# Turning weights and the first token pairs in 64-row halves, with another prologue order

## The reference

```python
x + attention(xn, ...) + ffn(xn, ...)
# ffn: one scalar per token and channel m (64 of them), 16 inner units each
s = xn @ Win + bin_                                  # [tokens, 64]
h = relu(s[..., None] * W1 + b1)                     # [tokens, 64, 16]
g = einsum('btmh,mh->btm', h, W2) + b2
ffn = g @ Wout + bout
# attention: q, k, v = projections of a second layer norm of xn (Wq, Wk, Wv),
# 16 heads of 32; its loops slice [:, :, :16], the first 16 tokens of each batch.
# Three rounds of: ql, kl, vl = small 32x32 projections of q, k, v; layer norms of
# ql and kl; softmax(ql kl^T); out = that @ vl; q += out; k, v = kl, vl.
attention = out.transpose(...).reshape(...) @ Wo.T + bo
```

## Time and profile before

| | |
|---|---|
| median of 3 runs (lowest, highest) | 303.13 us (302.8, 304.87) |
| profiled execution: its time, its span | 303.48 us, 301.7 us |
| busy: TensorE, VectorE, ScalarE, POOL | 276.4, 251.3, 219.9, 234.0 us |
| share of the span | 92%, 83%, 73%, 78% |
| DMA | 87.87 MB, mean 291 GB/s |
| mean granted TensorE clock | 0.979 |

### The profile page before, as it was taken

How to read it: one execution, slowest core, us unless ns; L and a number is a source line. 1 busy time by engine, 2 the same in 40 slices (tenths; PEclk the granted TensorE clock), 3 DMA queues, 4 the chain that set the end, 5 groups by cost and what they waited for, 6 DMA issues and landing times.

```text
span 301.7 us, 6220 instructions
## 1 busy us (share of the span) xinstructions
PE 276.4 (92%) x2371; PEld 116.1 (38%) x2371; DVE 251.3 (83%) x392; ACT 219.9 (73%) x260; POOL 234.0 (78%) x209
## 2 busy tenths in 40 slices
PE   4797498989999999899999999999989999999990
PEld 4652265524443432434443434434343333242220
DVE  0878484999997799998599987899999989967682
ACT  1546733873788699797979778898769797976910
POOL 8543109999679797979897897979793989899940
PEclk9999689997999999999999999999999999999998
...
GB/s 239 284 369 393 255 189 333 342 347 285 262 302 250 238 360 290 389 283 386 194 319 296 335 343 294 357 267 406 171 357 302 354 314 333 126 233 37 240 241 336
DMA packets 50573, 87.87 MB, mean 291 GB/s; under 512 B 6360, under 2 KB 35184, under 8 KB 46448
## 3 DMA queue, kind: packets, MB, share of 16 engines
...
...
## 4 chain that ended last, share of the span: by engine, by line
PE 61%; DVE 23%; issue 6%; POOL 3%; DMA 3%; ACT 1%; DVEq 0%; POOLq 0%; ACTq 0%
PE sg L594 14%; PE sg L537 13%; PE op L629 12%; DVE x L1048 6%; DVE stats L1092 5%; PE ra L556 4%; PE ra L629 3%; DMA b2c<-in_L_ffn_b_dram 3%; DVE xqT L1079 2%; PE op L352 2%; PE rb L483 1%; PE op L483 1%; PE ra L483 1%; PE ra L352 1%; PE A L326 1%
## 5 line engine op out<-in xcount | busy, mean ns | idle before, releaser
L1227 POOL TENSOR_TENSOR x<-x,bias_row 128x512 f32<-128x512 f32 x128 | 160.5, 1293 | 0.0
L1092 DVE BATCH_NORM_STATS2 stats<-x 128x6 f32<-128x512 f32 x128 | 80.7, 672 | 9.5 <-DMA x<-in_L_attn_x_dram 9.5
L816 ACT ACTIVATE H<-ra,b1c,w1c 128x1024 f32<-128x1024 f32 x64 | 72.8, 1205 | 9.4 <-PE rb L556 9.3
L816 ACT ACTIVATE H<-rb,b1c,w1c 128x1024 f32<-128x1024 f32 x60 | 68.9, 1220 | 3.0 <-PE sg L594 2.5
L594 PE MATMUL sg<-H,w2s 128*32 128x512 f32 x496 | 64.6, 616 | 3.0 <-ACT H L816 2.9
L1048 DVE TENSOR_TENSOR x<-x,op 128x1024 f32<-128x1024 f32 x46 | 55.7, 1212 | 13.3 <-PE op L629 13.2
L1211 POOL TENSOR_TENSOR rstd<-veps,nhalf 128x8 f32<-128x8 f32 x16 | 26.7, 1671 | 43.0 <-DVE veps L1104 42.9
L537 PE MATMUL sg<-xT,win 128*32 128x512 f32 x256 | 58.0, 595 | 1.3 <-ACT xqT L787 0.9
L629 PE MATMUL op<-wout,G 64*128 64x512 f32 x184 | 51.6, 637 | 2.2 <-DVE x L1048 1.9
L537 PE MATMUL sg<-xqT,winq 128*32 128x512 f32 x224 | 50.8, 595 | 0.0
L1079 DVE STREAM_TRANSPOSE xqT<-xq 128x1024 f32<-128x1024 f32 x28 | 34.6, 1234 | 2.2 <-DMA xq<-in_L_attn_x_dram 2.1
...
## 6 DMA issues: line engine op xcount, KB each, us to landing
out_dram<-x SPq DMA_DIRECT2D x30, 1024.0 KB, 6.8
...
x<-in_L_attn_x_dram SPq DMA_DIRECT2D x12, 1024.0 KB, 11.9
...
x<-in_L_attn_Wq_dram SPq DMA_DIRECT2D x1, 1024.0 KB, 19.0
x<-in_L_attn_Wk_dram SPq DMA_DIRECT2D x1, 1024.0 KB, 21.1
x<-in_L_attn_Wv_dram SPq DMA_DIRECT2D x1, 1024.0 KB, 7.4
```

The source lines that it names most:

```text
L816: act.activation(Hr[half][k % len(Hr[half])][:, :], rep_ps[half][:, :], ACT.Relu, bias=b1c[:, half, k:k + 1], scale=w1c[:, half, k:k + 1]) ...
L1092: dve.bn_stats(stats[:, j, :], x_sb[m][:, j * D:(j + 1) * D]).then_inc(bn_done, 1)
L1227: pool.tensor_tensor(x_sb[m][:, c], x_sb[m][:, c], bias_row[:, :], ALU.add).then_inc(xc_done, 1)
```

## The change

The four weights are loaded into x4 and x5 (Wq, Wk; Wv, Wo). The buffers WvT and WoT take the turned Wq and Wk first, and after `product_qk` the turned Wv and Wo. A unit now is eight tiles in sixteen 64-row halves, written to two banks (o_ps or RA_ps in turn); VectorE copies the first bank, ScalarE the second, for unit 0 VectorE both. There are 8 units instead of 16, and `product_qk` follows the fourth. `turn_first` turns the first two pairs the same way, four units for a pair, and `evacuate_first` copies 1024 columns at once.

The load of pair 3 waits for nothing any more, that of pair 4 for four units, that of pair 5 for eight. SP issues quads(2) and pair 3 right behind Wo. Thirteen small loads (bq, bv; three 32x32 weights, five vectors, three scalars) are issued by POOL: two between inv_std(0) and inv_std(1), eleven between inv_std(1) and inv_std(2). In the last attention round the kT product and its copy are left out, since nothing reads them. The tables of places are new, and VectorE takes the first three statistics of pair 4 one pair earlier, as it does from pair 5 on. The diff, its core:

```diff
-        w_nat = [x_sb[3 + i // 2 * 2][:, (i % 2) * DC * D:(i % 2 + 1) * DC * D].rearrange("p (c i) -> p c i", c=DC) for i in range(4)]
-        w_t = [t.rearrange("p (c o) -> p c o", c=DC) for t in
-               (x_sb[4][:, 0:DC * D], x_sb[4][:, DC * D:2 * DC * D], sb("WvT", [P, DC * D])[:, :], sb("WoT", [P, DC * D])[:, :])]
+        w_nat = [x_sb[4 + i // 2][:, (i % 2) * DC * D:(i % 2 + 1) * DC * D].rearrange("p (c i) -> p c i", c=DC) for i in range(4)]
+        w_t = [t[:, :].rearrange("p (c o) -> p c o", c=DC) for t in (sb("WvT", [P, DC * D]), sb("WoT", [P, DC * D]))]
+        w_t = w_t + w_t
...
+            if n == 4 and h == 0:
+                sp.wait_ge(turned, DC)
+            elif n == 5 and h == 0:
                 sp.wait_ge(turned, 2 * DC)
-            elif n == 4 and h == 0:
-                sp.wait_ge(qk_ps, 1)
-            elif n == 5 and h == 0:
-                sp.wait_ge(turned, 4 * DC)
...
             load_weight(2, Wv)
             load_weight(3, Wo)
+            load_quads(2)
+            load(3, 0)
+            load(3, 1)
             sp.dma_start(wout[0:M, :], Wout).then_inc(in_wo2, 16)
             sp.dma_start(wout[M:P, :], Wout).then_inc(in_wo2, 16)
-            for i, w in enumerate((Wlq, Wlk, Wlv)):
-                sp.dma_start(small[:, i * HD:(i + 1) * HD], w).then_inc(in_small, 16)
-            for i, v in enumerate((blq, blk, blv, lnc_w, lnd_w)):
-                sp.dma_start(small[:, 3 * HD + i:3 * HD + i + 1], col(v)).then_inc(in_small, 16)
-            sp.dma_start(bqc[:, :], bq.rearrange("(c p) -> p c", p=P)).then_inc(in_bq, 16)
-            sp.dma_start(bvc[:, :], bv.rearrange("(c p) -> p c", p=P)).then_inc(in_bq, 16)
-            for i, v in enumerate((temp, threshold, factor)):
-                sp.dma_start(scal[:, i:i + 1], v.partition_broadcast(P)).then_inc(in_scal, 16)
-            load(3, 0)
-            load(3, 1)
-            load_quads(2)
             load_quads(3)
             load(4, 0)
...
+        def weights_evacuated(count):
+
+            pe.wait_ge(turn_dve, count + 1)
+            if count > 1:
+                pe.wait_ge(turn_act, count - 1)
+
         def product_qk():
-            pe.wait_ge(turn_dve, DC)
...
-            for u in range(4 * DC):
-                i, ic = divmod(u, DC)
+            for u in range(2 * DC):
+                i, pair = divmod(u, 2)
                 yield next(AT_PE)
-                if ic == 0:
+                if pair == 0:
                     pe.wait_ge(in_w[i], 16)
                 if u == 0:
                     pe.wait_ge(R_done, 2)
+                elif u == 1:
                     pe.wait_ge(relu_done, HK)
-                if u >= NB:
-                    pe.wait_ge(turn_act if u % 2 else turn_dve, (u - NB) // 2 + 1)
-                for oc in range(DC):
-                    mm = pe.transpose(banks[u % NB][:, oc * P:(oc + 1) * P], w_nat[i][:, oc, ic * P:(ic + 1) * P], ident[:, :])
+                else:
+                    weights_evacuated(u - 1)
+                to = quarter_banks(turn_bank[u % 2])
+                for k in range(2):
+                    c = 2 * pair + k
+                    for oc in range(DC):
+                        for h in range(2):
+                            own = slice(h * M, (h + 1) * M)
+                            mm = pe.transpose(to[:, h, k, oc * M:(oc + 1) * M], w_nat[i][own, oc, c * P:(c + 1) * P],
+                                              ident[own, own], tile_position=(h * M, 0))
                 mm.then_inc(turned, 1)
-                if u == 2 * DC - 1:
+                if u == DC - 1:
...
+                if it < ROUNDS - 1:
+                    pe.matmul(A_ps[:, 0:CR], bd[:, 2, :], kT[:, :], start=True, stop=True)
                 pe.matmul(A_ps[:, CR:2 * CR], bd[:, 3, :], vT[:, :, 0, :], start=True, stop=True).then_inc(kv_ps, 1)
                 yield next(AT_PE)
                 pe.wait_ge(kv_made, it + 1)
...
 
-            return 2 * DC * min(n, BY_PE) + DC // 2 * max(0, n - BY_PE)
-
-        def first_bank(n, g):
-
-            banks = (o_ps,) if n == 1 and g >= DC else (RA_ps, RB_ps)
-            i = g % (2 * len(banks))
-            return banks[i // 2][:, i % 2 * BLK:(i % 2 + 1) * BLK]
-
-        def turn_first(n, g):
+            return DC * min(n, BY_PE) + DC // 2 * max(0, n - BY_PE)
+
+        def first_bank(n, i):
+
+            return ((RA_ps, RB_ps, o_ps, RA_ps), (RA_ps, RB_ps, o_ps, o_ps))[n][i]
+
+        def turn_first(n, i):
             m = n % RING
-            b, c = divmod(g, DC)
-            if c == 0:
+            b, pair = divmod(i, 2)
+            if pair == 0:
                 pe.wait_ge(*landed(n, b))
-            if n == 1 and g == DC:
+            if (n, i) == (0, 3):
+                pe.wait_ge(ev_done, 1)
+            elif (n, i) == (1, 0):
+                pe.wait_ge(ev_done, groups(1))
+            elif (n, i) == (1, 2):
                 pe.wait_ge(R_done, 1)
-            elif n == 1 and g < DC:
-                pe.wait_ge(ev_done, groups(n) - DC + g + 1)
-            else:
-                width = 2 if n == 1 else DC
-                if g >= width:
-                    pe.wait_ge(ev_done, groups(n) + g - width + 1)
-            for j in range(TILES):
-                col0 = b * HALF + j * D + c * P
-                mm = pe.transpose(first_bank(n, g)[:, j::TILES], x_sb[m][:, col0:col0 + P], ident[:, :])
+            elif (n, i) == (1, 3):
+                pe.wait_ge(ev_done, groups(1) + 3)
+            for k in range(2):
+                c = 2 * pair + k
...
+
+            return turn_bank[u % 2][:, h * D:(h + 1) * D].rearrange("p (k o x) -> p k o x", k=2, o=DC)
+
+        def turned_part(u, h):
+
+            i, pair = divmod(u, 2)
+            return w_t[i][:, 2 * pair:2 * pair + 2, :].rearrange("p k (o h x) -> p h k o x", o=DC, h=2)[:, h, :, :, :]
+
         def act_attention():
...
-                i, ic = divmod(u, DC)
+            for u in range(1, 2 * DC):
                 yield next(AT_ACT)
                 act.wait_ge(turned, u + 1)
-                act.activation(w_t[i][:, ic, :], banks[u % NB], ACT.Copy).then_inc(turn_act, 1)
-                if u == 2 * DC - 1:
+                if u >= DC:
+                    act.wait_ge(qk_ps, 1)
+                act.activation(turned_part(u, 1), turned_bank(u, 1), ACT.Copy).then_inc(turn_act, 1)
+                if u == DC - 1:
                     yield next(AT_ACT)
                     act.wait_ge(qk_ps, 1)
...
+                dve.wait_ge(turned, u + 1)
+                if u >= DC:
+                    dve.wait_ge(qk_ps, 1)
+                for h in range(2 if u == 0 else 1):
+                    dve.tensor_copy(turned_part(u, h), turned_bank(u, h)).then_inc(turn_dve, 1)
+
+            for u in range(DC):
                 yield next(AT_DVE)
-                dve.wait_ge(turned, u + 1)
-                dve.tensor_copy(w_t[i][:, ic, :], banks[u % NB]).then_inc(turn_dve, 1)
-
+                evacuate_weight(u)
             yield next(AT_DVE)
             dve.wait_ge(in_bq, 32)
...
             v = tick(dve.tensor_scalar(avg[:, :], block4[:, :], 1.0 / HD, None, ALU.mult))
             dve.wait_ge(dve_own, v)
             vc = tick(dve.tensor_tensor(centre[:, :], ident[:, :], avg[:, :], ALU.subtract))
+            for u in range(DC, 2 * DC):
+                yield next(AT_DVE)
+                evacuate_weight(u)
             yield next(AT_DVE)
             dve.wait_ge(dve_own, v)
...
             reach(side, 0, 22)
+            for j in range(3):
+                statistics(3, j)
+                reach(side, 0, 23 + j)
             for n in range(2, N):
...
                     turn_quads(n + 1, 0)
                 reach(side, n, 13)
-                if n > 2 and has(n + 2):
...
-            for n in range(3):
-                inv_std(n)
-                reach(side, 0, n)
+            inv_std(0)
+            reach(side, 0, 0)
+            for dst, v in ((bqc, bq), (bvc, bv)):
+                pool.dma_start(dst[:, :], v.rearrange("(c p) -> p c", p=P)).then_inc(in_bq, 16)
+            inv_std(1)
+            reach(side, 0, 1)
+            for i, w in enumerate((Wlq, Wlk, Wlv)):
+                pool.dma_start(small[:, i * HD:(i + 1) * HD], w).then_inc(in_small, 16)
+            for i, v in enumerate((blq, blk, blv, lnc_w, lnd_w)):
+                pool.dma_start(small[:, 3 * HD + i:3 * HD + i + 1], col(v)).then_inc(in_small, 16)
+            for i, v in enumerate((temp, threshold, factor)):
+                pool.dma_start(scal[:, i:i + 1], v.partition_broadcast(P)).then_inc(in_scal, 16)
```

106 lines of the change are left out of this document (52 added, 54 removed), and 3 rows, old and new, of the table AT_PE.

## The result

The changed kernel takes 305.07 us (median of 20 executions, 303.51 to 307.53), the kernel before 303.69 us beside it: 1.4 us more by the medians. The ratio is 1.0069, with a 95% interval of 1.0048 to 1.0090; that is 2.1 us. Predicted were 297.0 us, so the change costs 1 to 2 us where a gain of 6 was forecast. The profiled execution took 304.7 us, its span 302.9, against 303.48 and 301.7 before. The ratios leave out executions far above the fastest of the same kernel (also one of 392.99 us in the run with transposes), and the profiled execution of the run with both corrections was such a one, so no row of it is read.

The account below looks back on a forecast made before the run. TensorE was taken to bound the loop, so an earlier loop start should end the kernel earlier: 5.6 us at turn(2,0) plus 0.5 for the dropped product, 6.1 us, gives 297.4 profiled, 297.0 median; range 294.8 to 300.5.

Parts of the forecast that it names:

- step 4: VectorE's bqs, tile4, avg, centre before weight copies, 1 to 2 us hidden by product_qk; loop start stays 5.6 us earlier.
- a possible gain only: VectorE's small operations of pair 3 may meet POOL between adds, attention's places save waits: 293.5 to 295.5 us, chance 0.07.
- step 2: Prologue: first weight unit and sum_h before 34.5 us, copies behind quads; product_qk starts at 40.2 instead of 44.58, 4.4 us.
- step 3: From product_qk (3.65 us) through the later weight units: turn(2,0) at 47.05, stretch 3.2 instead of 4.43 us, gaining 1.2.
- step 7: Last round drops a kT matmul and its evacuation, 0.5 us of TensorE; moved attention places taken as zero.
- Step 1: variance(1) ahead of xn, bias_row, winq: spread_rstd(1) at 29.7 instead of 31.20, R there at 30.8, ReLUs from 31.2.
- the 35.22 that was counted with: VectorE's first quad transpose ahead of the weight copies waits for its load until 35.22 us, as before.
- the rival that had 0.17: TensorE at half clock around product_qk, up to 3.65 us lost; time 298.2 to 300.7 us, chance 0.17.
- Step 5: SP's quads(2) and load(3) at once behind Wo, there by 48.6; wout by 51.3, just ahead of 51.55: cost zero, tight.
- the 200 that it named: Sign for the loads: no rate under 200 GB/s from 40 to 46 us.
- Step 6: POOL issues thirteen small loads; bq and bv taken as 2.2 us each, 1.6 us late, 1.4 covered by the quads' wait.
- the rivals with 4.5 us and with 5.1 to 7 us: POOL's bq and bv issue: 4.5 us each, 301.8 us, chance 0.07; 5.1 to 7 each, some 307 at 7, chance 0.04.

Follow-up runs that it names:

- the run with transposes: Changed kernel plus 24 transposes of the identity into an unread bank ahead of product_qk: 305.43 us, ratio 1.0063 to the kernel before.
- the run with both corrections: Changed kernel with pair 0's bias adds ahead of inv_std(2) and pair 4's statistics in their old place: 300.36 us, ratio 0.9886.
- the last run: Changed kernel with only SP's load order altered (wout, load(3), quads(2)): 304.15 us, ratio 1.0009 to the kernel before.
- the run with the copies in front: Changed kernel, pair 0's adds early, pair 4's statistics back, VectorE's copies of units 1 to 3 ahead of pair 2's quads: 301.39 us.
- the run with SP's old order: Changed kernel, pair 0's adds early, pair 4's statistics back, small loads on SP again in the old order: 303.95 us, ratio 1.0019.
- the first run: Changed kernel with pair 0's eight bias adds ahead of inv_std(2): 301.53 us, ratio 0.9939 to the kernel before.
- the run with wout first: Changed kernel, pair 0's adds early, pair 4's statistics back, SP issuing wout, load(3), quads(2): 300.49 us, ratio 0.9917.

## Why the prediction was wrong

**The failed step** is the end of step 4, "the start of the loop stays at 5.6 us", with the sum's assumption that what comes earlier at turn(2,0) is there at the end. Adds in the prologue were looked at for the operations that the change moves (bqs to centre); the four of variance(3) stayed where they were and were named as a possible gain only, at 1.31 us each. They were a wait whose end is set by the quads' landing and POOL's row of adds, and not by turn(2,0). The runs showed it from two sides: moving the adds takes 3.9 us from the changed kernel and 2.2 from the one before, and then the product with `centre` follows turn(2,0) by 20.4 us or less; and with the adds in one row an earlier turn(2,0) (49.52, 48.51) is not there any more at that product, counted from the first add. Even with steps 2 and 3 as forecast the 5.6 us would have ended at this wait: 4.15 of them were there in the last run, and add(0,1) started 0.45 us earlier.

From 297.4 us, the forecast for the profiled execution, to its 304.7 are 7.3 us. 3.7 were lost ahead of turn(2,0) (50.74, not 47.05: 1.6 in step 2, 2.1 in step 3), 2.0 at the adds' wait (the lead of 1.92 at turn(2,0) became a lag of 0.09 at add(0,1)), 1.2 from there to the product with `centre` (step 7's statistic), and 0.4 of the 0.5 for the dropped product didn't show.

**Step 1** was short by 0.7 us, without an effect on the result. `spread_rstd(1)` came at 30.39, not 29.7, and ScalarE (answers to the earlier trace rows) copied R from 30.89 on, where it should have been there at 30.8; the four ReLUs began at 31.65, not 31.2:

```profile
30.89 0.60 ACT L806 ACTIVATE R<-op 128x512 f32<-128x512 f32 x1 [1.11 <-PE op L483]
...
31.65 4.50 ACT L824 ACTIVATE H<-rb,b1c,w1c 128x1024 f32<-128x1024 f32 x4
```

POOL's first operation of inv_std(1) began 1.8 us earlier than before but took 2.65 us instead of 1.65:

```profile
28.36 1.65 POOL L1211 TENSOR_TENSOR rstd<-veps,nhalf 128x8 f32<-128x8 f32 x1 [4.43 <-DVE veps L1104]
```

```profile
26.55 2.65 POOL L1226 TENSOR_TENSOR rstd<-veps,nhalf 128x8 f32<-128x8 f32 x1 [1.34 <-DVE veps L1116]
```

It now runs beside xn, bias_row and winq, VectorE's operations with two SBUF inputs that variance(1) was moved ahead of. The 2.63 to 2.65 us are in all eleven traces read here that have this order of VectorE, the 1.65 in both with the old one; that VectorE held POOL up here is an inference from that, since no run moves these three alone. The quads' wait (1.95 us at 35.62) covered the delay.

**Step 4, first half,** held: bqs to centre took 0.16 to 0.29 us each. So did the 4.48 us from turn(2,0) to project(0,0) (55.23 - 50.74).

**Step 2** was short by 1.6 us: product_qk at 41.77, not 40.2. The quads' loads are all of it: the first was turned 0.40 us later than the 35.22 that was counted with, the second waited 1.27 us (38.71), where none was counted. By the run with the copies in front, product_qk would come some 2.0 us earlier without the quads ahead of it.

**Step 3** was short by 2.1 us more: product_qk took 5.28 us, 1.6 of it by the half clock, the rival that had 0.17; the other 0.5 lie in the units behind it (3.69 us to turn(2,0), not 3.2). The clock's part is real (with transposes in the gap 3.59 us), but had no share in this result: the wait swallowed it.

**Step 5**, loads at no cost, held in the median for load(3) and wout: with wout first nothing was gained once the wait was gone. Its margin was as thin as said, with waits of 0.34 us for x here and 2.06 us for wout in one of the other executions. It didn't hold for the quads of pair 2, and the rate, 187 GB/s from 40 to 41 us, fell below the 200 that it named. Whether the denser loads behind the quads made them late, no run settles: in the run with SP's old order the second quads still waited 0.80 us.

**Step 6** held: bq and bv took 0.84 and 0.77 us to issue, less than the 2.2 taken, so the rivals with 4.5 us and with 5.1 to 7 us are out. Their landing mattered more than their issue (the run with SP's loads, 3.6 us).

**Step 7**: the places of the attention steps and of the statistics "move by a few; I take zero". One of them, the statistic ahead of add(0,3), cost 1.2 to 1.4 us while the adds' wait stood, because VectorE, busy without a gap from 61 us on, ends last there: the statistic itself is 0.6 us, and qkn then falls otherwise beside POOL's next adds (0.6 us more). In the traces with the adds early it makes no difference, 9.90 us from dmean to the product with it (the first run) and without it (the run with wout first). The 0.5 us of the dropped product are not seen: from the product with `centre` to the end it is 0.1 us. Whether the halves alone bring anything wasn't tried.
